# Early fusion, one layer: text tokens from tables of 34 rows, image blocks of 384 columns, state-space kernels summed by TensorE

## The reference

```python
pos = where(valid, j - last_sep + 2, 1)        # 1..33: a text row depends on its position alone
h = concat([patches @ W_proj.T + b + pos_emb, weights[pos]], axis=1)
x = layernorm(h)
u = x @ W_x.T + b_x ;  g = sigmoid(x @ W_g.T + b_g)
u = u * g + (conv3(u) + conv_b) * (1 - g)      # over L, per channel
dt = clip(softplus(x @ W_dt.T + b_dt).mean(all tokens), 0.001, 2.0)
A = -softplus(A_raw) ;  A_d = exp(A * dt) ;  B_d = (A_d - 1) / (A + 1e-6) * B_ssm
y[t] = sum_s C[s] * state[t, s],  state[t] = A_d * state[t-1] + B_d * u[t]
h = h + layernorm(x + y @ W_out.T + b_out)
h = h + moe_top2(layernorm(h))                 # 4 experts, unchanged code in both kernels
```

## Time and profile before

| | us |
|---|---|
| median of three runs (lowest, highest) | 497.39 (496.68, 498.31) |
| span of the profiled execution | 495.2 |
| TensorE busy, matmuls (weight loads) | 442.5 (363.4) |
| VectorE busy | 330.5 |
| ScalarE busy | 296.4 |
| GpSimd busy | 152.2 |

### The profile page before, as it was taken

How to read it: one execution, slowest core, us unless ns; L and a number is a source line. 1 busy time by engine, 2 the same in 40 slices (tenths; PEclk the granted TensorE clock), 3 DMA queues, 4 the chain that set the end, 5 groups by cost and what they waited for, 6 DMA issues and landing times.

```text
span 495.2 us, 9980 instructions
## 1 busy us (share of the span) xinstructions
PE 442.5 (89%) x3149; PEld 363.4 (73%) x3149; DVE 330.5 (67%) x980; ACT 296.4 (60%) x667; POOL 152.2 (31%) x255
## 2 busy tenths in 40 slices
PE   8989989799899999999999798999999999999400
PEld 5769967667778878887777577888878888888300
DVE  6885567678999434335786777866674666666584
ACT  2854359177975465316554354887786777877341
POOL 2000000000000000001243887874778644543322
PEclk9999999799999999999999999999999999999955
DMA  7981089900019942972511222232322333252262
GB/s 178 187 228 56 33 253 322 292 0 2 1 35 259 217 114 58 228 228 81 180 54 52 89 94 77 86 97 66 107 98 76 107 107 110 74 155 69 78 213 82
DMA packets 58734, 59.94 MB, mean 121 GB/s; under 512 B 25368, under 2 KB 51260, under 8 KB 57404
## 3 DMA queue, kind: packets, MB, share of 16 engines
q1 hardware_dynamic: 54236, 48.68, 36.4%
q0 software_dynamic: 3552, 9.74, 5.3%
q10 hardware_dynamic: 896, 0.89, 0.6%
HBM read 34.50 MB, written 24.80 MB: 120 GB/s over the span
## 4 chain that ended last, share of the span: by engine, by line
PE 66%; DVE 12%; issue 7%; ACT 7%; POOL 4%; DMA 2%; SPq 1%; DVEq 0%; POOLq 0%; ACTq 0%
PE bank L1040 14%; PE bank L881 9%; PE bank L433 8%; PE bank L435 8%; PE bank L434 8%; PE bank L955 3%; PE bank L1030 3%; PE bank L901 3%; POOL sorted_x L671 2%; PE bank L1012 2%; ACT U L470 1%; DVE spj L1400 1%; DMA got<-expert_y 1%; PE bank L848 1%; PE bank L947 1%
## 5 line engine op out<-in xcount | busy, mean ns | idle before, releaser
L1040 PE MATMUL bank<-w,hr 128*128 x320 | 76.0, 380 | 1.5 <-DVE ysb L1661 1.5
L1040 PEld LDWEIGHTS bank<-w,hr 128*128 128x128 f32 x320 | 60.1, 190 | 11.7 <-issue 2.7
L644 POOL MEMSET ones<- 2x128 f32 x1 | 0.2, 194 | 212.3 <-PE bank L916 212.3
L1234 ACT ACTIVATE hr<-bank,gsel 128x128 f32<-128x128 f32 x160 | 59.9, 460 | 0.2 <-PE bank L1030 0.2
L719 POOL DMA_INDIRECT expert_y<-ysb,toid x40 | 42.8, 1071 | 51.3 <-DVE ysb L1661 34.7
L881 PE MATMUL bank<-Tb,U 68*32 68x68 f32 x1024 | 45.9, 358 | 0.3 <-issue 0.3
L881 PEld LDWEIGHTS bank<-Tb,U 68*32 68x32 f32 x1024 | 40.6, 139 | 3.6 <-issue 3.1
L1646 DVE BATCH_NORM_STATS2 bsth<-bank 128x6 f32<-128x512 f32 x40 | 27.7, 693 | 20.5 <-PE bank L435 20.2
L671 POOL DMA_INDIRECT sorted_x<-x2s,slot x34 | 33.8, 994 | 15.3 <-issue 9.2
L1226 ACT ACTIVATE hn<-bank,nmrh,rsh 128x512 f32<-128x512 f32 x40 | 31.1, 777 | 10.0 <-DVE nmrh L1655 8.1
L433 PE MATMUL bank<-w_hi,bT_hi 128*128 x80 | 35.0, 438 | 0.1
(11 more groups left out here) (297 smaller groups left out, 1153.3 us busy)
## 6 DMA issues: line engine op xcount, KB each, us to landing
Tb<-ssm_kernels SPq DMA_DIRECT2D x16, 680.0 KB, 7.5
sorted_x<-zpad SPq DMA_DIRECT2D x6, 1419.0 KB, 13.6
xg<-sorted_x SPq DMA_DIRECT2D x40, 129.0 KB, 2.1
got<-expert_y SPq DMA_DIRECT2D x17, 256.0 KB, 3.6
XI<-in_x_dram SPq DMA_DIRECT2D x12, 288.0 KB, 5.6
h0r<-h_spill SPq DMA_DIRECT2D x17, 128.0 KB, 2.1
out_dram<-acc SPq DMA_DIRECT2D x17, 128.0 KB
w1raw<-in_L_ffn_w_dram SPq DMA_DIRECT2D x4, 512.0 KB, 15.9
```

Of the source, the lines that this page charges most:

```text
L1040: mm = pe.matmul(bank[6][:, 0:D], hr[:, i % 3, c, :], w2[:, bass.ds(expert[i], 1), c, :].rearrange("p o n -> p (o n)"), start=(c == 0), st ...
L1234: last = act.activation(hr[:, i % 3, c, :], bank[3 + i % 2][:, c * P:(c + 1) * P], ACT.Relu, scale=gsel[:, i, 0, c:c + 1], bias=gsel[:, i, ...
```

## The change

Blocks are now three of 384 columns (images) and two of 512 (text). Text tiles pass a1 only: their row is needed for the residual sum, and their statistics are taken per table row. All that the block computes of a text token before the state-space step depends on its position and on its two neighbours' positions, so it is taken from tables of 34 rows. A ring step `tab` normalizes and transposes the table and counts each row's tokens (for the mean of dt); steps `pt` project it by the three weights; from these come a table U of u, a table D of 3 x 34 rows (u less the convolution, one third for the token itself, one for each neighbour) and a table G of the gate's complement, each in high and low parts. A step `T` makes a quarter of a text block: six matmuls of 512 columns with the one-hot rows (OH now has 102 rows), a copy of the gate on ScalarE, and two instructions on VectorE. The mean of dt over the text is a weighted sum over 34 rows.

The cap of the exponential moves from VectorE to GpSimd, behind exp instead of before it. Taps are laid out with 8 channels x 16 states on the partitions, so weighting and summing become 64 matmuls of 68 weights' columns by 8 (`kT`); the product `dtr` spreads dt over that layout. VectorE makes three of the four exponent blocks, GpSimd one. VectorE now copies `kt` before the first convolution. Both runs of idle matmuls are gone. ScalarE loads its function tables three times instead of six before the second half. PSUM banks are renumbered.

```diff
-    BLOCKS = [(n, min(512, N - n)) for n in range(0, N, 512)]
+    NI = LI * B
+    VOC = LT + 2
+    NIB = 3
+    BLOCKS = [(n, NI // NIB) for n in range(0, NI, NI // NIB)] + [(n, 512) for n in range(NI, N, 512)]
     NB = len(BLOCKS)
+    NDT = HC * NIB
+    GH = P // S
+    NG = H // GH
...
-        PREP = [("pos", 0), ("pos", 1), ("vec",)] + [("wp", c) for c in range(0, CK, 2)]
+            return (BLOCKS[nb][0] + BLOCKS[nb][1]) // P
+
+        PREP = [("pos", 0), ("pos", 1), ("vec",)] + [("wp", c) for c in range(0, CK, 2)] + [("tab",)]
         IMAGES = [("img", half, g, wp) for g in range(2) for wp in range(HP) for half in range(2)]
         WEIGHTS = [("w", w, dc) for w in range(3) for dc in range(DC)]
-        A_RING = PREP + IMAGES + WEIGHTS
-        LAST_IMAGES = (len(PREP) + len(IMAGES) - 2, len(PREP) + len(IMAGES) - 1)
+        TABLES = [("pt", 0), ("pt", 1), ("pt", 2), ("tt", "U"), ("tt", "D")]
+        A_RING = PREP + IMAGES + WEIGHTS + TABLES
+        ring_hi = lambda q: sum(1 for step in A_RING[:q + 1] if step[0] in ("wp", "img", "w"))
+        TAB = PREP.index(("tab",))
+        W0 = len(PREP) + len(IMAGES)
+        PT0 = W0 + len(WEIGHTS)
 
         A_STEPS = [("ring", q) for q in range(len(PREP))]
-        ahead = list(range(len(PREP), len(A_RING)))
-        for k in range(NT + 3):
-            A_STEPS += [(f"a{s + 1}", TILE_ORDER[k - s]) for s in (3, 2, 1, 0) if 0 <= k - s < NT]
-            count = 3 if k < NH0 else 1
-            A_STEPS += [("ring", q) for q in ahead[:count]]
-            ahead = ahead[count:]
-            if k in (NT, NT + 1):
-                A_STEPS.append(("dt", k - NT))
-        assert not ahead
+        for n in range(len(IMAGES)):
+            A_STEPS.append(("ring", len(PREP) + n))
+            if n % 3 == 2:
+                A_STEPS.append(("a1", NTI + n // 3))
+        BESIDE = {1: [("ring", W0), ("ring", W0 + 1)], 2: [("ring", W0 + 2), ("ring", W0 + 3)],
+                  3: [("ring", W0 + 4), ("ring", W0 + 5)], 4: [("ring", PT0)], 5: [("ring", PT0 + 1)],
+                  6: [("ring", PT0 + 2), ("ring", PT0 + 3)], 7: [("ring", PT0 + 4)], 9: [("dt", 0), ("dt", 1)],
+                  10: [("dt", 2), ("dt", 3)]}
+        for k in range(NTI + 3):
+            A_STEPS += [(f"a{s + 1}", k - s) for s in (3, 2, 1, 0) if 0 <= k - s < NTI]
+            A_STEPS += BESIDE.get(k, [])
...
+        both = lambda j, nb: [("u", j, nb), ("g", j, nb)]
+
+        DT_STEPS = ([("zt",)] + [("dt", q) for q in range(6)] + [("Gt",), ("T", 0, 3), ("dt", 6), ("dt", 7), ("T", 0, 4),
+                    ("dt", 8), ("dt", 9), ("T", 1, 3), ("dt", 10), ("dt", 11), ("T", 1, 4)])
+
+        def woven(j, v0):
+            extra = text(j) + both(j, 0) + both(j, 1) + both(j, 2)
+            return [s for k in range(SV) for s in [extra[k]] + ssm(v0 + k, v0 + k + 1)]
...
-        C_STEPS = (proj(1, range(NB)) + turns(0) + [("kT",)] + proj(2, range(NB)) + ssm(0, 4) + turns(1)
-                   + ssm(4, SV) + woven(3, range(0, 2)) + turns(2) + woven(3, range(2, NB)) + [("wo", 0), ("wo", 1)]
+        C_STEPS = ([("u", 0, 0), ("u", 0, 1), ("dtr",), ("u", 0, 2), ("u", 1, 0), ("u", 1, 1), ("g", 0, 0), ("g", 0, 1),
+                    ("kT",), ("u", 1, 2), ("g", 0, 2)] + [("g", 1, nb) for nb in range(NIB)] + turns(0)
+                   + text(2) + both(2, 0) + ssm(0, 2) + both(2, 1) + ssm(2, 4) + both(2, 2) + ssm(4, 5) + turns(1) + ssm(5, SV)
+                   + woven(3, SV) + turns(2) + [("wo", 0), ("wo", 1)]
...
+            for q in range(NDT):
+                w = BLOCKS[q // HC][1]
+                pool.wait_ge(sem("dt_exp"), q + 1)
+                pool.tensor_scalar(spt[:, q % 4, 0:w], spt[:, q % 4, 0:w], 2.0 ** 57, None, ALU.min).then_inc(
+                    sem("dt_capped"), 1)
+
+            h0_out(pool)
+            pool.wait_ge(sem("zrow_stored"), 64)
+            pool.wait_ge(sem("adt"), 1)
+            powers_of(pool, 3, "adt_pool")
...
+                    elif kind == "tab":
+                        pe.wait_ge(sem("front"), front("tabx"))
+                        pe.wait_ge(sem("front"), front("hot1"))
+                        pe.wait_ge(sem("sort_consts"), 10)
+                        for dc in range(DC):
+                            pe.transpose(ps[:, dc * VOC:(dc + 1) * VOC], tabx[:, dc * P:(dc + 1) * P],
+                                         ident[0:VOC, 0:VOC])
+                        pe.matmul(ps[:, DC * VOC:(DC + 1) * VOC], onem[0:VOC, :], dg34[:], start=True, stop=True)
+                        for t in range(NH0):
+                            c0 = (DC + 1) * VOC + 2 * t
+                            mm = pe.matmul(ps[:, c0:c0 + 2], OH[0:VOC, t * P:(t + 1) * P].bitcast(F32), rnt[:],
+                                           start=True, stop=True)
+                    elif kind == "pt":
+                        w = rest[0]
+                        for j in range(HC):
+                            for dc in range(DC):
+                                mm = split3(pe, ps[:, j * VOC:(j + 1) * VOC], WT[w][0][:, dc, j * P:(j + 1) * P],
+                                            WT[w][1][:, dc, j * P:(j + 1) * P], tx_hi[:, dc, :], tx_lo[:, dc, :],
+                                            dc == 0, dc == DC - 1)
...
+            def chosen_rows(ps, hi, lo, j, nb):
+                n0, w = BLOCKS[nb]
+                rows_ = hi.shape[0]
+                at_ = OH[0:rows_, n0 - NI:n0 - NI + w]
+                pe.matmul(ps[:], hi[:, j * P:(j + 1) * P], at_, start=True, stop=False)
+                return pe.matmul(ps[:], lo[:, j * P:(j + 1) * P], at_, start=False, stop=True)
+
+            def project_text(j, nb):
+                freed(G_SEQ, ("G", j, nb))
+                if (j, nb) == (0, NIB):
+                    pe.wait_ge(sem("front"), front("gtab"))
+                    pe.wait_ge(sem("a_read"), len(A_RING))
+                chosen_rows(gbank(("G", j, nb)), tG_hi, tG_lo, j, nb)
+                freed(U_SEQ, ("D", j, nb))
+                chosen_rows(ubank(("D", j, nb)), tD_hi, tD_lo, j, nb).then_inc(sem("D_mm"), 1)
+                freed(U_SEQ, ("U", j, nb))
+                chosen_rows(ubank(("U", j, nb)), tU_hi, tU_lo, j, nb).then_inc(sem("U_mm"), 1)
...
-            pe.wait_ge(sem("v_init"), 4)
-            idle(bank[1], 20)
-            for q in range(AHEAD, HC * NB):
-                project_dt(q)
...
                 if step[0] == "kT":
-                    pe.wait_ge(sem("kernel_sum"), HC)
+                    pe.wait_ge(sem("front"), front("wsel"))
                     for j in range(HC):
-                        mm = pe.transpose(ps[0:L, j * P:(j + 1) * P], Kk[:, j, :], ident[:])
+                        pe.wait_ge(sem("powers"), j + 1)
+                        for g in range(j * NG // HC, (j + 1) * NG // HC):
+                            mm = pe.matmul(ps[0:L, g * GH:(g + 1) * GH], Eb[:, g, :], wsel[:, g, :], start=True, stop=True)
...
+                    dve.tensor_copy(g36[:, j % 2, :], gt2[:, n % 2, 0:B])
+                signal(dve.tensor_tensor(v, ubank(("D", j, nb))[:], gt2[:, n % 2, :], ALU.mult), "t_gated", n)
+                dve.wait_ge(sem("U_mm"), nth(U_SEQ, ("U", j, nb)))
+                dve.scalar_tensor_tensor(v, ubank(("U", j, nb))[:], vec[:, bx0 + j:bx0 + j + 1], v, ALU.add,
+                                         ALU.subtract).then_inc(sem("t_mixed"), 1)
...
-            def capped(q):
-                w, j = BLOCKS[BLOCK_ORDER[q // HC]][1], q % HC
-                dve.wait_ge(sem("dt_mm"), q + 1)
-                dve.tensor_scalar(spt[:, q % 4, 0:w], bank[4 + q % 4][:, 0:w], vec[:, bdt0 + j:bdt0 + j + 1], 40.0,
-                                  ALU.add, ALU.min).then_inc(sem("dt_capped"), 1)
...
-                dve.wait_ge(sem("powers"), j + 1)
-                link(dve.tensor_tensor(Eb[:, j], Eb[:, j], wmix[:, j].rearrange("p (o s) -> p o s", o=1).broadcast_to([P, L, S]),
-                                       ALU.mult))
-                dve.reduce_sum(Kk[:, j, :], Eb[:, j], AX).then_inc(sem("kernel_sum"), 1)
-
-            for j in range(HC):
-                kernel_sum(j)
+            for j in range(HC - 1):
+                powers_of(dve, j, "adt")
+            dve.wait_ge(sem("act_front"), act_front("wexp"))
+            link(dve.scalar_tensor_tensor(wmix[:], wmix[:], 1.0, wb[:], ALU.subtract, ALU.mult))
+            dve.wait_ge(sem("front"), front("by16"))
+            dve.tensor_tensor(wsel[:], wmix[:].rearrange("p (g o) -> p g o", o=1).broadcast_to([P, NG, GH]),
+                              by16[:].rearrange("p (o a) -> p o a", o=1).broadcast_to([P, NG, GH]), ALU.mult).then_inc(
+                                  sem("front"), 1)
+            q = C_RING.index(("kT",))
+            dve.wait_ge(sem("c_ps"), q + 1)
+            dve.memset(kt[L // 32 * 32:LR], 0.0).then_inc(sem("kt_ready"), 1)
+            dve.wait_ge(sem("kt_ready"), 1)
```

(1 more changed line is left out.)

693 lines of the change are left out of this document (435 added, 258 removed).

## The result

| us | before | after | forecast |
|---|---|---|---|
| median of four runs (lowest, highest) | 497.52 (496.68, 498.31) | 538.90 (535.52, 540.57) | 492, range 482 to 502 |
| span of the profiled execution | 495.2 | 535.1 | 489.9 |

The kernel after takes 1.082 times the time of before (95% interval 1.078 to 1.086): 8% slower, where I forecast 1% faster, and outside the range. The profiled execution took 537.81.

The account below looks back on a forecast made before the run. TensorE was taken to carry two thirds of the chain, VectorE bounding or sharing some stages. Stages of 37.8, 44.9, 29.6, 32.5 and 48.9 plus a tail of 296.2 gave a span of 489.9; 2.2 more made 492.1, range 482 to 502.

Parts of the forecast that it names:

- a, the front: Start to the first image product: forecast to end at 37.8 us instead of 34.16, +3.6.
- a wait of 3.65 was followed by half speed, which can cost 0 to 2.6; I add 0.9: Front, TensorE's wait ahead of `tab`: allowance of 0.9 us for half clock, from a wait seen in dt before.
- later than 22: Front: sign of being wrong if `tab` ended after 22 us; its end was put at 20.1.
- b, the image tiles: First image product to last split of a transposed tile: forecast 44.9 us, ending at 82.7, +14.3.
- c, dt: Mean step dt, last split to the end of adt: forecast 29.6 us, ending at 112.3, -8.7.
- 0.75, between them: dt: price in us of GpSimd's cap on 384 columns, between neighbouring rows giving 0.40 and 1.18.
- d, the kernels: End of adt to first u product of quarter 2: forecast 32.5 us, ending at 144.8; the 64 products 6.4.
- e: Quarters 2 and 3, to the end of the Wo transposes: forecast 48.9 us, ending at 193.7.
- Rival 3: TensorE stays at half speed through dt and the turns: 500.4 us (499 to 503), chance 0.26.
- seam d: End of the first u product of quarter 2: forecast 144.8 us; passing 150.1 was to decide for Rival 3.
- Rival 2: Full clock throughout, cheap 34- and 8-column products, GpSimd cap at 0.4: 488.6 us, down to 485.5; chance 0.22.
- Rival 4: The removed work was hidden anyway, first u product of quarter 2 at 150: 497.4 us within 1.5; chance 0.12.

Follow-up runs that it names:

- e1: Kernel after with 26 instead of 16 warming matmuls at the start and 16 idle matmuls ahead of `tab`; 538.43 us, 1.081 of the kernel before.
- e5: e1 plus 20 idle matmuls behind `tab`, ahead of the first image transposes; 523.97 us, 1.052 of the kernel before.
- e14: Kernel after with `tab` moved behind the images, no fills added; 522.22 us, 1.050 of the kernel before.
- e6: e5 plus a 376-column idle product between the quarters of each projected table, nine in all; 525.91 us.
- e9: e6 with the cap of exp(dt) moved from GpSimd back to VectorE; 522.62 us.
- e10: e6 plus 20, 14 and 8 idle products in three waits of dt; 520.31 us.
- e8: e6 with the first two convolutions of quarter 0 ahead of VectorE's wait for the kernels' products and copy; 524.65 us.
- e11: Kernel before without its 20 and 14 idle products; 497.20 us over ten runs, 0.998 of the kernel before.
- e13: Kernel after with all that helped: `tab` moved and mixed, wide products in tables, one-pass kernels, early convolutions, VectorE cap, dt fills; 507.80 us, 1.019 of before.
- e15: Kernel before plus 24 unused 34-column products ahead of each of three weight steps; 515.48 us, 1.030 of the kernel before.
- e7: e6 with the kernel products' operands in the rounded one-pass format; 521.33 us.
- e3: Kernel before with 6 instead of 16 warming matmuls, so that TensorE waits ahead of the one-hot product; 498.24 us, one run.

## Why the prediction was wrong

The span missed by 45 us, and by the readings below some 31 of it are TensorE at half clock: 15.7 in the front, 5.9 in the image tiles, 4.7 in dt, 4.8 in the kernels' products. I had allowed 0.9 and about 2.

**a, the front: the failing step is "a wait of 3.65 was followed by half speed, which can cost 0 to 2.6; I add 0.9".** I priced half clock as one spell of the length seen at 95.33, where dense 512-column products followed and won it back. In the ring nothing does: 13.8 in its eight groups and 1.9 in `tab`, instead of 0.9. I had also not asked what narrow products do, and so had the cause in the wrong place: with the wait bridged, `tab` itself sinks the clock (e1), and with wide products behind `tab`, or `tab` moved away, the ring holds full clock (e5, e14). The group at full clock, 2.12 for my 1.95, was a small miss, and the rest is that the ring began late: `tab` "later than 22" was one of my signs of being wrong, and it ended at 24.7.

**b, the image tiles: the mechanism was right and the sum near, the clock was missing.** At full clock the stage is 43.6 for my 44.9 (e6); the terms of my sum give 39.5 where I wrote 39.7. Three spells behind the tables, 16, 15 and 9 tile products at 0.21 instead of 0.12, are 3.9, and the end of the front's spell (to 60.8) 2.0: 5.9, where 5.3 is the difference found, so the clock is all of it.

**c, dt: two prices, and the clock.** The cap "0.75, between them" measured 1.18, the upper end from the earlier trace rows, 2.5 of dt by e9. Text products "0.227 for 512 columns" measured 0.33: six for 2.0 at 134.67 to 136.67, 24 in this stage, +2.5 of TensorE's time. The price was in my own text: 0.42 for the two one-hot products of a text row with 256 columns, where two tile products of 256 cost 0.26. I priced by columns and not by that. The rest was the half clock behind the three waits, 4.7 with e10, where I had allowed one spell of about 2. These overlap, for 7.1 in all; e9 and e10 were not run together without other changes.
The Trainium skill (GPSIMD Engine Reference, section 4.1) puts one-input work at roughly line rate, by which I had weighed a cheaper cap. It does not hold here: the one-input instruction over 384 columns took 1.18 against 0.35 on VectorE, 3.4 times as long.

**d, the kernels: "I take 0.10, near the loads: 6.4" measured 11.6**, and here too it was the clock. At full clock a product, in its two passes, costs 0.106, so 6.8; the fall to half clock in their midst adds 4.8, and some 2 in the products behind them. The price was right, if by luck: its source, a weight load of 0.09, is not what it consists of. That there were two passes could be read before. A state-space step is 16 matmuls (I wrote 64), and the four steps of the earlier trace rows stand there as 128 records, so that 0.041 was the price of a pass. "Powers three, 3.8" took 5.51 beside GpSimd's one, though four took 4.90 before: 1.84 each for 1.23. Either sharing or the new layout can be why; it was not tried apart. "VectorE holds everything behind it": e8 shows that this was worth 1.3 at most.

**e: the distance was 48.9 by count of columns and measured 54.2.** The text products' price is 12 x 0.1 of it; the rest fits a price on changes between groups of products with other weight rows (ten of text and projections at about 0.2, and eight more into state-space groups at 0.27), which I had counted in stage b and left out here. That sum, 5.4 for 5.3, is from rows after the fact; it is not shown, and a change of weight rows alone was not tested.

**The rivals.** Rival 3 had the right mechanism (half clock) at the wrong place and far too small: 500.4 with 0.26. Its test, "a granted clock under 0.8 from 82 to 140", comes out 0.77 and 0.80 in dt and the kernels, but the loss in the front was in no rival. That seam d passed 150.1 (183.1) decides nothing for it, as the front alone moved it there. Rival 2 is refuted by 0.112, 0.106 and 1.18. Rival 4 is refuted: stage c did fall by 16. e11 shows that the dropped fills, by which I argued for rival 3, had been worth nothing where they stood.

**Open.** Why the ring at half clock doesn't win it back though it does hold full clock; whether few rows of weights lower the clock as few columns do (e13, and the stretch of e1 above); what sinks it in the mixed `tab` of e13; what e15 waited for at 174.34; why a text product costs 0.33, since 102 rows alone don't do it.

## What to carry to other kernels

Before replacing wide products by many narrow ones, ask what runs behind them: count their own price, and then price everything up to the next long dense run at half clock, since that cost 14 us here behind a step of 4, and the narrow run itself too, if it is long: the kernels' products lost 4.8 of 11.6. Put unavoidable narrow products directly ahead of dense ones and not ahead of a mixed ring (in a→b a projected table cost 0.9 to 1.5 that way), and read the granted clock in windows, not only the busy share: 98% busy at 0.50 looks healthy in every view of busy time. For an unseen instruction take the nearest row by rows of weights, operand type and engine, and count the records of a row against the products of the program, since they may differ by two.

## What the runs showed of the hardware

- A run of narrow products without any gap took the granted clock from 1.00 to 0.50: 24 of 34 columns in e15, 20 passes of 2 and 34 columns in e1. A wait of 3.65 did so before. With products of 8 columns it fell inside their run (1.00 until 152.6 in after, 0.50 from 153.6).
- A ring of transposes of 96 columns and one 512-column product per step stayed at 0.50 for 29 us (e1) and at 1.00 for 17 (e5, e14). Dense 256-column products won it back in 5 us (55.97 to 60.8); products of 384 and 512 columns in dt did so after 7 us in after and after 16 in e1, with the same code.
- A product of plain fp32 operands stands as two records: 128 for 64 products, and 64 in the rounded format (e7). Such a pass with 8 columns took 0.053 at full clock and 0.09 at half.
- GpSimd's one-input minimum over 128x384 took 1.18, the same on VectorE 0.35; its fill of 128x512 took 0.525.
- A pair of one-hot products of 34 or 102 weight rows and 512 columns took 0.66 at full clock, 0.2 more than two 512-column products of 128 rows.
- In the first microseconds the granted clock may be recorded as 1.00 while products stand at half pitch: in e3 two 512-column products and four transposes took 1.89 (8.16 to 10.05) in a window recorded at 1.00, and the same six took 0.96 in the kernel before (10.06 to 11.02).
